# A graph network of four residual layers on one NeuronCore: another order of loads and masks at the opening, and small work spread over more steps of the second layer

## The reference, cut to what matters

```python
# layer 0 and layer 2: additive attention
Wh = h @ W;  s1 = Wh @ a1;  s2 = Wh @ a2
e = leaky_relu(s1[:, :, None] + s2[:, None, :], 0.2)
attention = softmax(e + where(adj == 0, -1e9, 0), axis=2)
out = elu(attention @ Wh)
# layer 1: a softmax over the neighbours for each feature
feat = softplus(x * (INV_SQRT2 * w0) + b0);  scores = feat * wa + ba
out = masked softmax of scores over j, times feat, summed over j
# layer 3: two rounds of dot product attention (four heads, then one), adj + identity as mask
x = _layernorm(x + layer(x, adj))
```

## Time and profile before

| | us |
|---|---|
| median of 3 runs (2028.95 to 2029.56) | 2029.12 |
| the profiled execution | 2027.78 |
| its span | 2025.5 |
| opening, to the first multiply of the first layer | 49.2 |
| one regular step of the second layer | 11.4 |
| mean granted clock of TensorE over the span, of full speed | 0.978 |

### The profile page before, as it was taken

The page is one execution under the profiler, slowest core; times in us unless marked ns, Lnnn a source line. Parts: engine busy times, 40 slices in busy tenths (PEclk is TensorE's granted clock), DMA queues, the critical chain, the costliest instruction groups (busy, mean ns, idle before and its releaser), DMA issues.

```text
span 2025.5 us, 51832 instructions
## 1 busy us (share of the span) xinstructions
PE 1912.5 (94%) x22356; PEld 1190.5 (59%) x22356; DVE 1624.3 (80%) x1914; ACT 1246.0 (62%) x2296; POOL 589.6 (29%) x443
## 2 busy tenths in 40 slices
PE   6999878999999799999999999999999999999983
PEld 4888766777888544555545545545455455454542
DVE  2999967887999887788888788888887888888863
ACT  2677766654877676566565665665656656656552
POOL 0233347873333300123122121231221212312215
PEclk7999989998999999999999999999999999999996
DMA  6000000000000001010110100101101001011010
GB/s 173 4 4 3 3 1 1 1 1 2 3 4 3 3 12 32 13 28 12 38 27 12 39 22 18 28 12 38 28 12 39 22 17 28 12 38 27 12 45 15
DMA packets 50363, 42.19 MB, mean 21 GB/s; under 512 B 33112, under 2 KB 36760, under 8 KB 50136
## 3 DMA queue, kind: packets, MB, share of 16 engines
q1 hardware_dynamic: 47752, 38.33, 6.9%
q10 hardware_dynamic: 2384, 0.56, 0.2%
HBM read 25.76 MB, written 4.72 MB: 15 GB/s over the span
## 4 chain that ended last, share of the span: by engine, by line
PE 58%; DVE 4%; POOL 1%; issue 1%; ACT 0%; DMA 0%; SPq 0%; ACTq 0%
PE fourth_ps_out L1517 22%; PE fourth_ps_scores L1467 7%; PE fourth_ps_out L1532 6%; PE fourth_ps_scores L1470 5%; PE fourth_ps_scores L1473 5%; DVE fourth_weights L1178 3%; PE fourth_ps_scores L1491 2%; PE fourth_ps_prep L1432 2%; PE fourth_ps_prep L1442 2%; PE fourth_ps_scores L1494 1%; PE fourth_ps_scores L1500 1%; PE fourth_ps_scores L1497 1%; PE fourth_ps_prep L1424 1%; DVE fourth_cat L1157 1%; PE fourth_ps_prep L1401 1%
## 5 line engine op out<-in xcount | busy, mean ns | idle before, releaser
L1178 DVE TENSOR_TENSOR fourth_weights<-fourth_weights,keep_mask 128x1024 f32<-128x1024 f32 x512 | 666.0, 1342 | 108.9 <-ACT fourth_weights L1336 107.1
L1336 ACT ACTIVATE fourth_weights<-fourth_ps_scores 128x1024 f32<-128x1024 f32 x512 | 497.0, 1024 | 347.4 <-PE fourth_ps_scores L1473 326.0
L1517 PE MATMUL fourth_ps_out<-fourth_weights,fourth_x_stage 128*64 128x512 f32 x2048 | 498.2, 605 | 4.9 <-DVE fourth_weights L1178 4.9
L612 DVE SCALAR_TENSOR_TENSOR additive_weights<-additive_ps_row,additive_gain,keep_mask 128x1024 f32<-128x1024 f32 x256 | 319.2, 1267 | 4.2 <-ACT additive_ps_row L727 4.2
L845 PE MATMUL additive_ps_out<-additive_values,additive_weights 128*64 128x65 f32 x8192 | 282.6, 225 | 27.0 <-DVE additive_weights L612 23.7
L845 PEld LDWEIGHTS additive_ps_out<-additive_values,additive_weights 128*64 128x64 f32 x8192 | 257.8, 139 | 49.4 <-DVE additive_weights L612 37.0
L1517 PEld LDWEIGHTS fourth_ps_out<-fourth_weights,fourth_x_stage 128*64 128x64 f32 x2048 | 124.2, 136 | 251.6 <-issue 216.3
L1467 PE MATMUL fourth_ps_scores<-fourth_g_high,fourth_x_high 64*128 64x512 f32 x1024 | 229.5, 445 | 2.1 <-ACT fourth_weights L1336 2.1
L1467 PEld LDWEIGHTS fourth_ps_scores<-fourth_g_high,fourth_x_high 64*128 64x128 f32 x1024 | 95.9, 183 | 200.7 <-issue 102.2
L1470 PE MATMUL fourth_ps_scores<-fourth_g_high,fourth_x_low 64*128 64x512 f32 x1024 | 202.1, 391 | 0.0
L1473 PE MATMUL fourth_ps_scores<-fourth_g_low,fourth_x_high 64*128 64x512 f32 x1024 | 201.5, 389 | 0.0
(11 more groups left out here) (210 smaller groups left out, 2790.5 us busy)
## 6 DMA issues: line engine op xcount, KB each, us to landing
fourth_recip_wide<-recip_out SPq DMA_DIRECT2D x128, 128.0 KB, 2.9
opening_adj<-in_adj SPq DMA_DIRECT2D x8, 512.0 KB, 8.0
fourth_h_high<-fourth_h_high SPq DMA_DIRECT2D x32, 128.0 KB, 2.7
fourth_h_low<-fourth_h_low SPq DMA_DIRECT2D x32, 128.0 KB, 2.4
out<-keep_x SPq DMA_DIRECT2D x16, 256.0 KB, 2.6
dens_out<-fourth_mixture SPq DMA_DIRECT2D x64, 4.0 KB
keep_x<-in_x ACTq DMA_DIRECT2D x1, 512.0 KB, 18.5
fourth_dens<-dens_out SPq DMA_DIRECT2D x32, 8.0 KB, 1.6
```

Of the source, the lines that this page charges most:

```text
L612: dve.scalar_tensor_tensor(out=weights[t % RING][:, :], in0=ps_row[s][:, :], scalar=gain[s][:, t:t + 1], in1=keep.mask[:, t, :].bitcast(F3 ...
L1178: dve.tensor_tensor(buf, buf, keep.mask[:, st.t, cols(half)].bitcast(F32).unsqueeze(1) .to_broadcast([P, 2, HALF]), ALU.mult).then_inc(wei ...
L1336: act.activation(weights[st.slot + half][:, :], ps_scores[half][:, :], ACT.Exp)\
L1517: last = pe.matmul(ps_out[rows(g), cols(half)], x_stage[st.s][:, st.t, g, :], weights[st.slot + half][:, cols(g)], start=(st.t == 0), stop ...
```

## The change

Six things change, and all instructions of the computation stay except those named.

1. ScalarE's queue loads batch 0 of `x` alone and first, ahead of W and the attention columns. SP's queue loads batches 1 to 3 after the adjacency, and batches 4 to 15 at its end.
2. VectorE's mask instruction also adds up each row (`accum_out`), which gives the degrees. From them it makes `empty_wide`, 128 x 8 x 128, in one instruction, eight matmuls with the identity (L470 of the changed kernel) turn it, and VectorE makes `keep.empty` before the first `weigh`. The 16 matmuls by the mask and `find_empty` beside batch 0 go away.
3. The first layer's weights are made one tile later (`copy_w` after mask tile 1, `copy_products` after tile 3), and the first chain of batch 0 comes one to three places later in each list.
4. The second layer's `preparation` hooks move from steps 0 to 7 to steps 3 to 12, with `copy_w` and `multiply_w` two steps apart in their order (4 on VectorE, 5 on TensorE), and `copy_twice` split in two.
5. The late norm of the first layer moves from steps 0 to 3 to steps 0 to 7.
6. Waits on `empty_ready` count to 2, since `empty_wide` counts too.

```diff
-    def copy_twice():
+    def copy_heads():
...
+    def copy_output():
...
-        if k == 1:
+        if k == 4:
             copy_w(1, third_w())
-        if k == 2:
+        if k == 6:
             copy_products(1, third_products())
+        if k == 7:
+            copy_heads()
+        if k == 8:
+            copy_output()
+        if k == 10:
+            copy_even()
+        if k == 12:
+            copy_odd()
+
+    def tensor(k):
         if k == 3:
-            copy_twice()
+            turn_w(1, third_w())
         if k == 5:
-            copy_even()
-        if k == 7:
-            copy_odd()
-
-    def tensor(k):
-        if k == 0:
-            turn_w(1, third_w())
-        if k == 1:
             multiply_w(1, third_products())
-        if k == 4:
+        if k == 9:
             multiply_even()
-        if k == 6:
+        if k == 11:
             multiply_odd()
...
-    degree = turned[0]
+    degree = mem.sbuf("degree", [P, TILES])
+    empty_wide = mem.sbuf("empty_wide", [P, TILES, P])
...
-        sp.dma_start(keep.x[:, 2:6, :, :], x_rows(ins)[:, 2:6, :, :]).then_inc(keep.x_loaded[0], 16)
+        sp.dma_start(keep.x[:, 1:4, :, :], x_rows(ins)[:, 1:4, :, :]).then_inc(keep.x_loaded[0], 16)
...
-        sp.dma_start(keep.x[:, 6:BATCH, :, :], x_rows(ins)[:, 6:BATCH, :, :]).then_inc(keep.x_loaded[1], 16)
+        sp.dma_start(keep.x[:, 4:BATCH, :, :], x_rows(ins)[:, 4:BATCH, :, :]).then_inc(keep.x_loaded[1], 16)
...
             dve.wait_ge(loaded[t], 16)
-            dve.tensor_scalar(rows[:, t, :], adj[:, t, :], 0.0, None, ALU.is_gt).then_inc(masked, 1)
-            if t == 0:
+            dve.tensor_scalar(rows[:, t, :], adj[:, t, :], 0.0, 0.0, ALU.is_gt, ALU.add,
+                              accum_out=degree[:, t:t + 1]).then_inc(masked, 1)
+            if t == 1:
                 weights.copy_w(0, first_w)
-            if t == 2:
+            if t == 3:
                 weights.copy_products(0, first_products)
-            if t == 5:
-                additive.find_tile_top(0)
-            if t == 6:
-                additive.find_minus_top(0)
-                additive.find_top(0)
-        additive.copy_tops(0)
+        dve.wait_ge(masked, TILES)
+        dve.tensor_scalar(empty_wide[:, :, :], degree[:, :].unsqueeze(2).to_broadcast([P, TILES, P]), 0.0, None,
+                          ALU.is_equal).then_inc(empty_ready, 1)
+        additive.find_tile_top(0)
+        additive.find_minus_top(0)
+        additive.find_top(0)
         dve.wait_ge(turned_full, TILES)
         dve.tensor_copy(keep.mask[:, :, (TILES - 1) * P:],
                         turned[1][:, :].rearrange("j (t i) -> j t i", i=P)).then_inc(last_copied, 1)
+        additive.copy_tops(0)
+        dve.wait_ge(consts, 11)
+        dve.wait_ge(empty_full, 1)
+        dve.tensor_scalar(keep.empty[:, :], turned[0][:, :], row_used[:, 0:1], None, ALU.mult).then_inc(empty_ready, 1)
...
+        act.dma_start(keep.x[:, 0, :, :], x_rows(ins)[:, 0, :, :]).then_inc(keep.first_x_loaded, 16)
         load_additive(act, 0, "L0_gnn_W", "L0_gnn_a")
-        act.dma_start(keep.x[:, 0:2, :, :], x_rows(ins)[:, 0:2, :, :]).then_inc(keep.first_x_loaded, 16)
...
-            if i == 3:
+            if i == 4:
                 additive.copy_x(0)
-            if i == 5:
-                additive.copy_hidden(0)
-                additive.copy_mean(0)
+        additive.copy_hidden(0)
+        additive.copy_mean(0)
...
         pe.wait_ge(copied, TILES - 1)
-        pe.wait_ge(last_copied, 1)
-        for j in range(TILES):
-            for h in range(HALVES):
-                last = pe.matmul(degree[:, h * HALF:(h + 1) * HALF], keep.ones_r[:, :],
-                                 keep.mask[:, j, h * HALF:(h + 1) * HALF],
-                                 start=(j == 0), stop=(j == TILES - 1))
-        last.then_inc(degree_ready, 1)
+        pe.wait_ge(empty_ready, 1)
+        for t in range(TILES):
+            last = pe.matmul(turned[0][:, t * P:(t + 1) * P], empty_wide[:, t, :], keep.ident[:, :],
+                             start=True, stop=True)
+        last.then_inc(empty_full, 1)
...
     def turn_x(b):
-        if b == 2:
+        if b == 1:
             pe.wait_ge(keep.x_loaded[0], 16)
-        if b == 6:
+        if b == 4:
             pe.wait_ge(keep.x_loaded[1], 16)
...
-        if (k, at) == (1, 1):
+        if (k, at) == (2, 1):
             additive.gpsimd_late(0, 1)
-        if (k, at) == (3, 0):
+        if (k, at) == (6, 1):
             additive.gpsimd_late(0, 2)
...
-        if (k, at) == (1, 0):
+        if (k, at) == (2, 0):
             additive.vector_late(0, 2)
-        if (k, at) == (2, 0):
+        if (k, at) == (3, 0):
             additive.vector_late(0, 3)
-        if (k, at) == (3, 0):
+        if (k, at) == (6, 0):
             additive.vector_late(0, 4)
...
-        if k == 0:
-            if at == 2:
-                additive.scalar_late(0, 0)
-                additive.scalar_late(0, 1)
-        if (k, at) == (2, 2):
+        if (k, at) == (0, 2):
+            additive.scalar_late(0, 0)
+        if (k, at) == (1, 2):
+            additive.scalar_late(0, 1)
+        if (k, at) == (4, 2):
             additive.scalar_late(0, 2)
-        if (k, at) == (3, 2):
+        if (k, at) == (7, 2):
             additive.scalar_late(0, 3)
```

32 lines of the change are left out of this document (12 added, 20 removed).

## The result

The changed kernel takes 2009.37 us (median of 4 runs, 2008.34 to 2012.24) against 2029.03 us (4 runs, 2024.57 to 2029.56): a ratio of 0.9907, 95% interval 0.9892 to 0.9921, so 19.7 us less, with 16 to 22 in the interval. Forecast were 2018.1, 11.0 less, with a range from 2012.0 to 2024.0. Three executions (2360.79 us of the kernel before, 2647.64 and 3630.05 of two experiments) ran in a slow state and are in no median and no ratio here.

A forecast was written before the change was run, and what follows sets the result against it. It took VectorE to bound the first layer and, with one ScalarE wait, the second layer's steps; early second-layer steps had 14.4 us extra. Opening 4.0 plus second layer 7.0 made 11.0, so 2029.1 becomes 2018.1, range 2012.0 to 2024.0.

The forecast's parts named there:

- Part 1: Opening, the loads: x lands by 13 us, the weights behind it at 17.5 (13.5 to 20), where the opening resumes.
- The bound of 9 for x: Opening: lower bound for x's landing, 0.8 + 2 + 6.2 = 9 us, against 13 if shared with the adjacency.
- Part 2: Opening, from the weights at 17.5 to the scores' tops: tops at 37.0 against 38.2 before, 40.2 at half clock.
- Part 3: Opening, tops to first multiply: at 43.6 against 49.2, 5.6 us won at full clock, up to 4.4 less if it falls.
- I take 4.0: Whole opening: 4.0 us won, ends -2 (weights at 20, half clock) and 7.
- Part 4: Second layer: stalls go, copying work stays; 7.0 of 14.4 extra us go, ends 4 and 9.5.
- the four with their own times: Rivals: poor opening 2021.1 (0.27), more gain 2012.6 (0.10), stalls back elsewhere 2026.1 (0.07), late weights making it slower 2031.6 (0.04).
- more than forecast: Rival, opening and second layer: x and weights early, clock full, work hidden, 7 + 9.5 = 16.5, 2012.6 us; chance 0.10.

The follow-up runs named there:

- the order alone: Changed kernel with the loads of the kernel before (weights first, two batches of x behind them): 2010.88 us, ratio 0.9912; a second time 2013.54 us, 0.9932.

## Why the prediction was right or wrong

**Part 1 failed, in both its numbers.** "13 if sharing with the adjacency costs one batch two thirds more, which I take": x landed 4.9 us after its issue at 0.77. The step took the pace of two batches behind the weights and at the height of the adjacency load for that of one batch ahead of everything. From this came "they land at 13 + 4.5 = 17.5" for the weights; VectorE had them at 10.36, 0.9 us later than before. The bound of 9 for x was the nearer one, and even that took the 12.4 us of rows 7 for the queue's own need, where it was the need of a queue in company. 7.1 us of the opening are here.

In the trace the opening's misses add up like this: the forecast is 7.1 us too late in this part, 3.9 more in Part 2, less 1.4 in Part 3, which makes the 9.6 between 43.6 and 33.95. Then 4.1 are lost again before the first reciprocal, which no part had. That the order alone (old loads, x at 21.59) was worth 10.1 us of medians once and 4.2 the second time shows that the early landing is not the only thing that gave the opening its gain: the shorter chain of Parts 2 and 3 gave a good share of it.

By the Trainium skill (DMA: Bandwidth & Descriptors, Queues, rings and completion order) a DMA engine goes round the queues that have work and changes only at packet boundaries, some 9 to 17 descriptors apart. The near one-to-one alternation of small and large packets agrees with going round; how long the turns are the DMA records, which don't name the engine, can't show, and the 880 packets beside 32, where x came first, are no even turns at all.

**Part 2 had the right chain and the wrong clock.** "TensorE then has at half clock (it idled before) four tiles at 1.97": since nothing stopped the engines until 17.5, half clock lasted only from 13.1 to 16.5 there, and the four tiles took 1.29, 3.03 (two of them) and 1.04 us. From `copy_w` to the tops I allowed 19.5 us and 15.6 were needed (17.0 in the two other traces of the changed kernel). The mask instruction with a sum took 1.22 + 0.08, as assumed (1.29).

**Part 3 was nearly right until the first multiply.** From tops to first `multiply` 6.6 forecast, 8.0 measured: 1.2 of the 1.4 are the half clock from 30.1 to 33.5, which the prediction had named as its risk (from L794 to the first `multiply` 4.7 us instead of 3.6). In the two other traces the clock stayed full there, and it is 6.4. L469's 6.24 us went off the path and L470's 1.95 stayed beside ScalarE's work, as said. Not foreseen was what came behind: 2.4 us of wait and 1.6 of half clock (91 matmuls in 4.48 us; in the kernel with x behind the weights, at full clock, 91 took 2.90):

```profile
42.51 2.90 PE L845 MATMUL additive_ps_out<-additive_values,additive_weights 128*64 128x65 f32 x91 [2.72 <-issue]
```

The opening's gain was 11.2 at the first reciprocal and 10.5 in the runs; with "I take 4.0" it was outside even my own upper end of 7.

**Part 4 was right:** 7.0 forecast, 7.5 in the trace, 8.2 in the runs; steps 2 and 3 take 11.3 and 13.2, though one is over the 12.5 I gave them. Steps 5 and 11 take 12.2, as said; step 8 takes 13.4, over the 13, because `copy_heads` (L236, four copies) takes 3.43 us of VectorE there, where I had priced it at 1.2.

**The rivals.** None of the four with their own times came; the nearest was "more than forecast", 2012.6 with a chance of 0.10, which took the opening to be worth 7 at most. It named the right direction, x and weights early and the clock full, and stopped at a bound that Part 1 had made too tight. Part of the miss was masked by the wait near 43 us: without the 4.1 us that the trace loses there, the forecast would have been further off.

## What to carry to other kernels

The time of a transfer read from a trace holds for its place: how long it took behind others and beside others says little of how long it takes first and alone. Bound it by the bytes ahead of it and in flight with it, and let the range reach down to nothing in company.

Taking out one wait of a crowded stretch moves part of it to the next step; look at the step behind before counting the gain. And a large load that is in nobody's way can still hold up the loads of the engines' own instructions. In a profile it shows as a busy engine that stands still with "issue" behind it and an instruction queue that moves nothing. Moving the load earlier or cutting it in four removed the wait here, though neither made the kernel measurably faster.
